# The third layer's turn with the full-height products together, the product with gamma on GpSimd and two products behind later additions

## The reference, cut to what matters

```
hidden = conv1x1(x, w_hidden) + b_hidden          # 48 -> 288 channels
qkv    = depthwise3x3(hidden) + b_dw              # q, k, v of 96 channels each
out    = irfft2(rfft2(q patches 8x8) * rfft2(k patches 8x8))
normed = (out - mean over channels) / sqrt(var over channels + 1e-5)
normed = normed * gamma + beta
return conv1x1(v * normed, w_out) + b_out
```

## Time and profile before

| | |
|---|---|
| median of 3 runs | 13274.48 us (13271.14 to 13285.16) |
| profiled execution, its own time | 13280.52 us |
| its span | 13277.9 us |
| granted TensorE clock, mean | 0.98 |
| busy over the span: PE, DVE, ACT, POOL | 96%, 62%, 42%, 35% |
| turns of the third layer | 256 |

### The profile page before, as it was taken

How to read it: one execution, slowest core, us unless ns; L and a number is a source line. 1 busy time by engine, 2 the same in 40 slices (tenths; PEclk the granted TensorE clock), 3 DMA queues, 4 the chain that set the end, 5 groups by cost and what they waited for, 6 DMA issues and landing times. The chain is left out here.

```text
span 13277.9 us, 324877 instructions
## 1 busy us (share of the span) xinstructions
PE 12696.7 (96%) x130266; PEld 8373.2 (63%) x130266; DVE 8260.9 (62%) x17483; ACT 5521.4 (42%) x11157; POOL 4651.8 (35%) x3557
## 2 busy tenths in 40 slices
PE   7999999899989998999999999999998999999998
PEld 6877444677767775444444444444446788788777
DVE  0000677433335444777777777777776777777777
ACT  0000111211123333444444444444445666667666
POOL 0000222000000254555555555555552443434433
PEclk9999999999999998999999999999999999999999
DMA  4333566883754696555555555555552222222222
GB/s 127 134 132 123 138 160 160 158 154 77 153 125 152 169 228 140 77 77 77 77 77 77 78 78 77 77 77 77 77 71 66 51 51 53 53 53 52 52 49 50
DMA packets 2284445, 1306.11 MB, mean 98 GB/s; under 512 B 1877860, under 2 KB 2176219, under 8 KB 2197359
## 3 DMA queue, kind: packets, MB, share of 16 engines
q1 hardware_dynamic: 2015884, 1183.10, 44.9%
q10 hardware_dynamic: 267232, 104.65, 3.3%
HBM read 646.90 MB, written 450.74 MB: 83 GB/s over the span
## 5 line engine op out<-in xcount | busy, mean ns | idle before, releaser
L1578 PE MATMUL l_m<-l_wa,l_pix 128*128 128x288 f32 x8192 | 2484.8, 426 | 18.0 <-DMA l_left<-k_within_dram 17.9
L1440 POOL TENSOR_TENSOR l_qkv<-l_qkv,l_copies 128x576 f32<-128x576 f32 x1024 | 1438.4, 1405 | 2044.0 <-DVE l_qkv L1781 2044.0
L1578 PEld LDWEIGHTS l_m<-l_wa,l_pix 128*128 128x128 f32 x8192 | 1390.4, 189 | 984.5 <-issue 766.5
L1287 PE MATMUL l1h_ps<-l1h_ring,l1h_w 96*96 96x256 f32 x6120 | 1328.7, 379 | 48.5 <-ACT l1h_ring L1235 46.1
L1058 PE MATMUL l1v_ps<-l1v_rows,l1v_w 96*96 96x256 f32 x6120 | 1326.3, 378 | 31.3 <-ACT l1v_rows L1031 31.3
L2099 PE MATMUL l_e<-k_ident,l_turn 128*112 128x128 f32 x9900 | 1164.5, 276 | 94.2 <-DVE l_out L2261 88.6
L2099 PEld LDWEIGHTS l_e<-k_ident,l_turn 128*112 128x112 f32 x9900 | 1086.6, 135 | 257.7 <-issue 128.2
L1287 PEld LDWEIGHTS l1h_ps<-l1h_ring,l1h_w 96*96 96x96 f32 x6120 | 999.7, 163 | 377.5 <-issue 46.5
L1430 POOL TENSOR_TENSOR l_pix<-l_raw 128x516 f32<-128x516 f32 x1024 | 1218.3, 1190 | 24.1 <-DMA l_raw<-l_raw 24.1
L1058 PEld LDWEIGHTS l1v_ps<-l1v_rows,l1v_w 96*96 96x96 f32 x6120 | 990.7, 162 | 366.6 <-issue 30.3
L1271 POOL TENSOR_TENSOR l1h_columns<-l1h_blocks,l1h_ring 96x2048 f32<-96x2048 f32 x64 | 356.3, 5591 | 2418.2 <-DVE l1h_ring L1320 2418.2
(11 more groups left out here) (245 smaller groups left out, 21993.9 us busy)
## 6 DMA issues: line engine op xcount, KB each, us to landing
l0a_x<-x_px_dram SPq DMA_DIRECT2D x128, 1176.0 KB, 5.0
l0b_x<-x_in_dram SPq DMA_DIRECT2D x128, 493.8 KB
l_raw<-l_raw SPq DMA_DIRECT2D x128, 483.6 KB, 7.2
l_raw<-x_dram SPq DMA_DIRECT2D x1280, 48.0 KB, 3.7
l_x<-x3p_dram SPq DMA_DIRECT2D x132, 384.0 KB
l_out<-x_dram SPq DMA_DIRECT2D x528, 96.0 KB
out_dram<-l_out SPq DMA_DIRECT2D x132, 384.0 KB
x_dram<-l0b_out ACTq DMA_DIRECT2D x256, 193.5 KB, 3.1
```

The lines of the kernel that those rows point to most:

```text
L1287: last = nc.tensor.matmul(ps[g][0:C2, 0:GI * V], w[:, kernel, s, :], ring[:, g, before % DEEP, :, s:s + V], start=(s == 0), stop=(s == 2))
L1440: nc.gpsimd.tensor_tensor(q, q, copies[:, g % 2, 1:2, :].broadcast_to([128, 2, OUTC]), ALU.add)\
L1578: return nc.tensor.matmul(bank[i][:, 0:OUTC], pix[:, k, i, first:first + 128], wa[:, b, i, :], start=(i != 3), stop=(i == 3))
```

## The change

- In `filters`, all four centres come first and then all four rests; bank 3 is now begun by its centre like the others.
- The second transpose of a half block (`turn_pixels(.., 1)`) moves on TensorE from the end of a turn to behind the first spectrum of the next one, and its copy on ScalarE (`read_turned(.., 1)`) from the turn's start to behind `read_k(p - 1, 3)`.
- The product `ya` = y * gamma goes from DVE to GpSimd (`times_gamma`), in groups 1 and 3, between `transform` and `add_second`.
- On DVE, `yb` and `t` of the first half move from behind `products(p - 1, 3)` to behind `add_first(p, j, 1)` and `products(p, 0)`, and those of the second half from ahead of `add_first(p, j, 3)` to behind `products(p, 2)`, which ends the turn.

```diff
+            def times_gamma(q, g):
+                pool.wait_ge(y_out, 2 + 2 * q + g + 1)
+                if q > 0:
+                    pool.wait_ge(yb_out, 2 * q + g - 1)
+                nc.gpsimd.tensor_tensor(ya[:, g], y[:, g], gb[:, 0], ALU.mult).then_inc(ya_out, 1)
...
                 for g in range(4):
                     if p < TOTAL - 2:
                         transform(p // 2 + 1, p % 2, g)
+                    if g % 2 == 1 and 1 <= p <= TOTAL:
+                        times_gamma(p - 1, g // 2)
                     if p < TOTAL:
                         add_second(p, p % PAIRS, g)
...
                 def centre(i):
                     return nc.tensor.matmul(bank[i][:, 0:OUTC], pix[:, k, i, first:first + 128], wa[:, b, i, :],
-                                            start=(i != 3), stop=(i == 3))
+                                            start=True, stop=False)
...
-                                            start=(i == 3), stop=(i != 3))
-                for i in (1, 2, 0):
+                                            start=False, stop=True)
+                for i in (1, 2, 0, 3):
                     if 4 * p + g > 0:
                         pe.wait_ge(freed[i], 4 * p + g)
                     centre(i)
-                if 4 * p + g > 0:
-                    pe.wait_ge(freed[3], 4 * p + g)
-                for i in (1, 2, 0):
+                for i in (1, 2, 0, 3):
                     rest(i).then_inc(conv_done, 1)
-                rest(3)
-                centre(3).then_inc(conv_done, 1)
...
                 if before:
                     spectrum(p - 1, j - 1, 3)
+                if last:
+                    turn_pixels(p - 2, 1)
...
                     inverse(p, 0)
-                if before:
-                    turn_pixels(p - 1, 1)
...
-                if last:
-                    read_turned(p - 2, j - 2, 1)
                 if before:
                     deviation(p - 1, 0)
                 if now:
                     read_conv(p, 0)
                 if before:
                     read_k(p - 1, 3)
+                if last:
+                    read_turned(p - 2, j - 2, 1)
+                if before:
                     normalise(p - 1, 0)
...
             def times_v(q, j, g):
-                dve.wait_ge(y_out, 2 + 2 * q + g + 1)
-                nc.vector.tensor_tensor(ya[:, g], y[:, g], gb[:, 0], ALU.mult).then_inc(ya_out, 1)
                 dve.wait_ge(ya_out, 2 * q + g + 1)
                 nc.vector.tensor_tensor(yb[:, g], ya[:, g], gb[:, 1], ALU.add).then_inc(yb_out, 1)
...
                 if before:
                     products(p - 1, 3)
-                    times_v(p - 1, j - 1, 0)
                 if now:
                     add_first(p, j, 1)
                     products(p, 0)
+                if before:
+                    times_v(p - 1, j - 1, 0)
                 if last:
                     residual(p - 2, j - 2)
...
                 if last:
                     count(p - 2, j - 2)
-                if before:
-                    times_v(p - 1, j - 1, 1)
                 if now:
                     add_first(p, j, 3)
                     products(p, 2)
+                if before:
+                    times_v(p - 1, j - 1, 1)
```

## The result

The changed kernel takes 13778.74 us (median of 4 runs, 13777.52 to 13789.24) and the kernel before 13279.82 (4 runs, 13271.14 to 13288.33): ratio 1.0377, 95% interval 1.0359 to 1.0395, so 3.8% slower. The forecast was 13,802 with a range of 13,480 to 14,000 and 0.84 for slower. The profiled execution took 13789.24, its span is 13787.4, and the mean granted clock 0.979.

What follows compares the result with a forecast made beforehand. A closed chain through ScalarE's root was to replace TensorE as the bound: halves of 10.26 and 10.27 plus 0.14 give 20.67 us a turn against 18.61. Over 256 turns that is 527 us more: 13,802, range 13,480 to 14,000.

Steps and rivals of the forecast that it cites:

- TensorE's part: On TensorE, one block of one shape fewer per group saves 4 x 0.20 = 0.80 us a turn, 205 us in all.
- The times at which `yb` and `t` end: On DVE, `yb` ends at A + 0.42, `t` at A + 1.79, or A + 1.97 and A + 2.97 in second halves.
- A: The time at which GpSimd's addition is over, from which the ends of `yb` and `t` on DVE are counted.
- GpSimd is not first behind an addition: Denies the rival that GpSimd keeps the port at every hand-over: 0.56 us more a turn, 13,946; chance 0.18.
- DVE is not first behind the copy: Denies the rival that DVE gets in at every hand-over, between copy and transform too: 20.05 us a turn, 13,643; chance 0.12.
- The closed chain: Loop through TensorE, ScalarE, DVE and GpSimd in both halves of a turn, setting the pace at 20.67 us; chance 0.48.
- to the end of `t`: Chain term on DVE from the end of GpSimd's addition: 1.79 us in the first half, mean 2.47 in the second.
- to the next copy of m1: Chain term through `residual`, variance and ScalarE's root: 2.24 us in the first half, 1.57 without `residual` in the second.
- the step from root to copy: On ScalarE, within the chain: the root takes 0.30 us, then 0.04 passes until the copy of m1.
- Gamma: GpSimd's product `ya`, taken as 0.94 us; it adds 0.14 to the chain in the second half, nothing in the first.
- what PE waits for: PE's waits for ScalarE's `l_copies` were to rise to some 700 us, and its busy time to fall to about 86%.
- The other side: Rival: `yb` and `t` find GpSimd at rest, TensorE keeps its pace, 13,070, or 13,223 straight after the addition; chance 0.13.

Runs made afterwards that it cites:

- e7: Kernel before with only the change's TensorE and ScalarE parts, plus SyncE issuing the first copies of `left` ahead of those of `mid`: 13109.42, 0.9863.
- e4: Whole change, plus two waits on GpSimd so that it lets DVE finish `t` in each half first: 13419.31, 1.0095.
- e8: e4 plus SyncE issuing the first copies of `left` ahead of those of `mid`: 13245.83, 0.9965.
- e10: Whole change, plus SyncE issuing the first copies of `left` ahead of those of `mid`, nothing else: 13775.15, 1.0363.
- e1: Kernel before with only the change's TensorE and ScalarE parts; DVE and GpSimd as before: 13142.69, 0.9888.
- e2: Kernel before with only the change's DVE and GpSimd parts; TensorE and ScalarE in the old order: 14631.28, 1.1006.
- e3: Whole change with `yb` and `t` back at their old places on DVE, gamma still on GpSimd: 13426.29, 1.0101.
- e12: e3 plus SyncE issuing the first copies of `left` ahead of those of `mid`: 13392.89, 1.0075.
- e6: Whole change with ScalarE's root (`deviation`) moved behind `read_conv` of groups 0 and 2: 13803.7, 1.0384.
- e9: Whole change with TensorE's old order in each group (three centres, four rests, then centre 3): 13767.78, 1.036.
- e5: Whole change with gamma's product back on DVE, directly ahead of `yb` at its late place: 14275.64, 1.074.
- e11: e6 plus SyncE issuing the first copies of `left` ahead of those of `mid`: 13561.1, 1.0203.

## Why the prediction was right, step by step

**TensorE's part: right, 0.80 us a turn.** e7 measures a turn of 17.82 for 17.81. In time it is 179 us (13288.22 to 13109.42) of the 205, since about half of the turns take 17.96: the mean of 247 is 17.88, where it was 18.61 before, and 256 x 0.73 = 187. The Trainium skill ("TensorEngine Tiling (Array Packing)", Key Properties) has the drain at a change of mode, and the trace agrees that such a change costs time, 0.20 us; the 0.05 us a group that the prediction estimated from the skill's pages is too small.

**The times at which `yb` and `t` end, right to 0.01 us in these turns.** `yb` ended at A + 0.42, `t` at A + 1.79 and A + 2.97, and in the turns without a copy at A + 1.97 (8001.86 to 8003.83). That decides between the rivals: GpSimd is not first behind an addition, and DVE is not first behind the copy. The second is against the rule of the Trainium skill ("SBUF — State Buffer", SBUF: two separate sides) that whoever starts first holds the pair, if it is taken by arrival: `t` is there from 8022.50 on and GpSimd's transform, which starts at 8023.33, still goes ahead. e4 and e8 show that the wait is on the chain.

**The closed chain, right.** By the same steps as in the forecast:

| term | forecast | first half | second half, with copy |
|---|---|---|---|
| centres to rests | 2.14 | 2.13 | 2.14 |
| to the copy of m1 | 0.79 | 0.79 | 0.78 |
| to the end of DVE's additions | 1.27 | 1.27 | 1.27 |
| to A | 1.58, with gamma 1.72 | 1.59 | 1.74 |
| to the end of `t` | 1.79 / 2.97 | 1.79 | 2.97 |
| to the next copy of m1 | 2.24 / 1.57 | 2.09 | 1.43 |
| copy to centre | 0.45 | 0.44 | 0.45 |
| sum | 10.26 / 10.91 | 10.10 | 10.78 |

**Mis-sized, the step from root to copy.** The sum had 0.34 from the root's start to the copy's. It is 0.20 where ScalarE had waited for the root's input (8015.48 to 8015.68): -0.14 in each half. In the earlier trace rows the copy starts 0.34 after the root, but PE's rests of that group start at 8009.52, and 0.78 after them is 8010.30: it waited for them and not for the root. **Gamma** took 1.00 and not 0.94, and holds the second half's addition up by 0.18 (it starts 0.35 after DVE's end and not 0.17) where 0.14 stood in the sum. So two turns are 20.88 + 19.88, mean 20.38 where 20.67 was forecast. That alone would be 74 us under the forecast.

**Left out, a cost of some 45 us.** The mean of 218 turns of this trace (5,400 to 9,900 us) is 20.56, because some are longer. Three of them, with 10 us in all, hold DVE's summary of an image, 1.88 us ahead of the variance. Eight others, with 17 us, have a wait for `left` and then a stretch at the lower clock. The remaining 12 us or so are steps of about 0.3 in some thirty turns, which are not explained. One turn of the first kind and one of the second, in the timeline of the changed kernel:

```profile
7917.92 1.88 DVE L1849 BATCH_NORM_AGGREGATE l_mvx<-l_stats 112x2 f32<-112x384 f32 x1
...
7921.61 3.45 PE L1586 MATMUL l_m<-l_wa,l_pix 128*128 128x288 f32 x8 [2.77 <-ACT l_copies L1676]
```

```profile
6127.70 4.21 PE L1586 MATMUL l_m<-l_wa,l_pix 128*128 128x288 f32 x8 [2.19 <-DMA l_left<-k_within_dram]
```

The first took 23.25 us: the chain has no slack for the 1.88, and the centres behind the wait of 2.77 take 3.38 (to the rests at 7924.99) at a granted clock of 0.62. The second took 25.38, with a granted clock of 0.50 from 6127.70 to 6135.50. 256 x (20.56 - 20.38) = 46 us, and in all 256 x (20.56 - 18.61) = 499 us, as the medians differ.

**Luck in the number.** The forecast of 13,802 lies 23 us above the 13,779 measured. The steps that were sized too long made it 74 too high, and the longer turns that were left out made it some 45 too low, so that most of the one error is cancelled by the other.

**Wrong, what PE waits for.** The waits were to be all for `l_copies`, some 700 us; over the whole layer PE's idle time ahead of the centres is 547.8 us, of which 345.0 ends with `l_copies`, and from 7000 to 9000 us a third of the waits is for `l_left` (70.1 against 132.8). The step that lacks is SyncE's queue: `residual` ends later in the turn, and the copies of `left` are behind a wait for it. e10 shows that it costs the change nothing, e4 and e8 that it costs 174 us where the chain is shorter. PE's busy share is 90% and not 86%. Part of that is how it is counted: a block's end is modelled and lies beyond the start that the next one could have (rests last 0.77, and the next block starts 0.70 after them), so every pause is shown shorter than it is. By the turns' lengths, 20.56 with pauses and 17.88 without (e7), the pauses are 2.7 us of a turn, 13%: an estimate of 87% for the busy share, near the 86.

**The other side was not near.** For a kernel no slower than before, both waits behind A would have had to fall from 4.26 to 2.20, and for TensorE's pace to 1.40 (4.26 - 2.86). In the turns shown they are 1.79 and, on average, 2.47. With `t` at A + 1.0 and the queue out of the way (e8) the kernel takes 13,246, near the 13,223 that the prediction gave for this case, and is at 0.9965; 0.35% is less than the 1.5% that TensorE's pace would give.

**What the chain did not tell.** It says what the change costs, and little of what a further edit wins. Of the twelve runs, the results of four (e1, e7, e8, e10) lay within what was expected; the other eight were all slower than the range given for them. Where the rows show why, it was something beside the chain: a transpose that ended the turn (e2), gamma's place in GpSimd's program (e3, e12), SyncE's queue (e4, e6), copies and products that were busy elsewhere (e9), an addition that took 1.75 (e5). What held e11 is open.

## What to carry to other kernels

Placing a DVE product behind an addition "of the same group" sets it beside GpSimd's longest operation; look on the other engine's timeline at the very moment in which it will run, since two such products in a row were over 1.8 to 3.0 us behind that operation, for 1.1 of work. When work moves later, follow every queue that has a wait for it (here SyncE's copies and ScalarE's root), and the rare long instruction too. Take the parts of a change one at a time but don't add them up: the part worth keeping (TensorE and ScalarE, with SyncE's copies reordered) gives 0.9863, while the other half alone is at 1.1006.

## What was not expected of the hardware

A single pause of PE can be followed by a stretch at the lower clock, and that can cost more than the pause. Behind 2.50 us for `left` in e6 the granted clock was 0.50 (1.2 GHz) for 7.8 us, which by half the time costs an estimated 3.9. Behind 2.19 in the change it was 0.50 for as long. Behind 3.11 in e2 it was 0.56 in a window of 3.6 us, and behind 2.77 in the change 0.62 in 3.4 us, which in the same way costs an estimated 1.6 and 1.3. It is not the length of the pause alone. In the change, centres at 7940.66 waited 2.47 us, and the window behind them (7940.60 to 7943.00) has 1.00. In e10 a wait of 1.18, with one of 0.79 some 2 us ahead of it, was enough for 0.58 in the window from 8301.00 to 8304.60:

```profile
8301.01 3.68 PE L1593 MATMUL l_m<-l_wa,l_pix 128*128 128x288 f32 x8 [1.18 <-ACT l_copies L1683]
```

What decides is open.

GpSimd's copy of the rows took 1.37 in place of 1.03 in the turn shown: `yb`, held until the addition ended, ran in its first part (until 8022.47). That is the same as with the transform of the earlier trace rows, 1.41 in place of 1.10. So the operation that is passed at a hand-over is slowed, by 0.31 to 0.34 us. The addition of 1.75 in e5 is another matter: the product on DVE ended 0.41 behind it, so it was not passed, and took 0.34 longer all the same. And a ScalarE operation behind the root starts 0.20 after it, though the root lasts 0.30; the next copy in turn starts 0.29 after one of 0.39. These operations overlap by 0.10, where the prediction put 0.04 between them.
